# A new order of the first stage's parts on four engines and the DMA queue, and one semaphore per decay buffer

## What is computed

```
h = layernorm(x) * (1 + ca) + sa;  x = x + ga * attention0(h)   # 16 query heads in 4 groups, width 16,
h = layernorm(x) * (1 + cb) + sb;  x = x + gb * (h @ w.T + bias) #   RMS norm and rotation of q and k, causal softmax
h = layernorm(x) * (1 + ca) + sa;  x = x + ga * attention1(h)   # 16 heads of 128, exponential decay by distance
h = layernorm(x) * (1 + cb) + sb;  x = x + gb * (experts(h) + shared(h))   # the best 2 of 8 experts
```

## Time and profile before

| | us |
|---|---|
| median of 3 runs | 1146.86 |
| lowest, highest | 1146.69, 1147.84 |
| the profiled execution, its own time | 1147.24 |
| its span, first to last instruction | 1145.5 |
| first stage, last work ends (B low of batch 2) | 239.05 |
| shift writes end, groups 0, 1, 2, 3 | 41.77, 54.94, 66.25, 81.01 |
| groups 4, 8, 12, 15 | 91.03, 140.55, 190.90, 225.43 |
| granted clock of TensorE, mean (1 is full speed) | 0.968 |

### The profile page before, as it was taken

One profiled execution on the slowest core, in us unless ns is written; L12 is line 12 of the kernel. 1 busy time (PEld: TensorE's weight loads), 2 busy tenths in 40 slices (PEclk: granted clock), 3 DMA queues, 4 the chain that ended last, 5 costly groups with the idle time before them and its releaser, 6 DMA issues. The chain is left out here.

```text
span 1145.5 us, 22304 instructions
## 1 busy us (share of the span) xinstructions
PE 1055.6 (92%) x7524; PEld 919.3 (80%) x7524; DVE 896.3 (78%) x1816; ACT 734.0 (64%) x1398; POOL 334.2 (29%) x335
## 2 busy tenths in 40 slices
PE   5988888869999999999999999999999997979994
PEld 4756666658899899899899898898898986769992
DVE  5798988856788788788788788788788787857765
ACT  4679797766766666666666666666666763615650
POOL 3353544442311201211211111111111244753440
PEclk9799999989999999999999999999999998989997
DMA  7210001010401311321311311221221292834426
GB/s 255 94 52 16 15 6 56 2 50 23 135 20 52 112 46 47 106 46 51 101 50 52 98 53 53 97 54 53 86 65 54 91 37 100 329 99 120 124 89 225
DMA packets 70264, 92.13 MB, mean 80 GB/s; under 512 B 22609, under 2 KB 50385, under 8 KB 69170
## 3 DMA queue, kind: packets, MB, share of 16 engines
q1 hardware_dynamic: 66786, 81.83, 25.7%
q0 software_dynamic: 3408, 9.39, 2.2%
HBM read 46.35 MB, written 42.75 MB: 78 GB/s over the span
## 5 line engine op out<-in xcount | busy, mean ns | idle before, releaser
L1551 PE MATMUL all_psum<-all_h_parts,attn_wp 128*128 128x512 f32 x1140 | 296.2, 395 | 0.0
L1551 PEld LDWEIGHTS all_psum<-all_h_parts,attn_wp 128*128 128x128 f32 x1140 | 209.1, 188 | 39.5
L1723 ACT CAST attn_pp<-attn_p 128x512 fp32r<-128x512 f32 (+3 forms) x256 | 117.4, 459 | 188.4 <-DVE attn_p L1831 186.2
L1812 DVE TENSOR_TENSOR attn_pp<-attn_p,attn_pp 128x512 fp32r<-128x512 f32 (+3 forms) x256 | 198.0, 773 | 6.5 <-ACT attn_pp L1723 6.5
L1970 POOL TENSOR_TENSOR all_gate<-all_gate,attn_sq 128x512 f32<-128x512 f32 x64 | 84.7, 1324 | 368.6 <-ACT attn_sq L1734 368.5
L1630 PE MATMUL all_psum<-attn_qkp 128*128 128x512 f32 (+3 forms) x768 | 164.6, 323 | 3.7 <-DVE attn_qkp L1812 3.7
L1577 PE MATMUL all_psum<-attn_pp,attn_vp 128*128 128x512 f32 (+3 forms) x768 | 163.3, 321 | 1.1 <-DVE attn_pp L1812 0.5
L1577 PEld LDWEIGHTS all_psum<-attn_pp,attn_vp 128*128 128x128 f32 x768 | 128.9, 189 | 21.6 <-issue 1.5
L1630 PEld LDWEIGHTS all_psum<-attn_qkp 128*128 128x128 f32 x768 | 124.1, 189 | 12.4 <-issue 4.3
L1831 DVE TENSOR_TENSOR attn_p<-all_psum,attn_mask 128x512 f32<-128x512 f32 (+3 forms) x256 | 123.4, 482 | 3.6 <-PE all_psum L1630 2.5
L1054 DVE TENSOR_REDUCE front_top<-all_psum 128x2 f32<-128x256 f32 (+3 forms) x128 | 99.3, 814 | 16.4 <-PE all_psum L695 15.1
(11 more groups left out here) (375 smaller groups left out, 1892.9 us busy)
## 6 DMA issues: line engine op xcount, KB each, us to landing
...
```

The costliest lines, as they stand in the source:

```text
L1551: last = nc.tensor.matmul(out, wp[:, a, k, col:col + P], hh[:, c, k, b * S:(b + 1) * S], start=(m == 0), stop=(m == 5))
L1723: nc.scalar.copy(pp[:, u % 2, 0, cols], p[:, cols]).then_inc(p_hi, 1)
L1812: nc.vector.tensor_tensor(out, whole, high.bitcast(F32), ALU.subtract).then_inc(ready, 1)
```

## The change

The tables and the two strings get other values. The parts and their instructions are the same ones. The semaphore `stored` becomes ten, one for each decay buffer; a wait for all stores becomes ten waits, and the wait before a buffer is written again is for that buffer's own store. The diff (the hunks that follow the tables are whole):

```diff
-PROLOGUE_AT = {"L stats": (0, 0), "L rstd": (0, 0), "L norm": (0, 10), "xt": (0, 13), "pj0": (0, 17), "pj1": (0, 17),
-               "sq": (1, 1), "ss": (1, 9), "std": (1, 12), "krot": (1, 13), "rms": (1, 14), "qn": (1, 18),
-               "rot": (2, 0), "va": (2, 8), "rope": (2, 11), "kt": (2, 12), "qt0": (2, 17)}
-POST_AT = {"A add": (0, 0), "at": (0, 7), "A rstd": (0, 11), "out": (0, 12), "A stats": (0, 18), "A norm": (1, 8),
-           "ta": (1, 14), "A low": (1, 16), "bias": (1, 17), "B add": (2, 4), "ff": (2, 11), "B stats": (2, 14),
-           "B rstd": (2, 16), "B low": (3, 3), "B norm": (3, 7), "tb": (3, 14)}
-FIRST_AT = {"dec12": (0, 0), "diag0": (0, 0), "dec10": (0, 4), "dec11": (0, 6), "dec13": (1, 8), "dec14": (1, 19),
-            "diag1": (2, 0), "diag2": (2, 4), "gb0": (2, 8), "gb1": (2, 16), "w ffn": (3, 1), "diag3": (3, 2),
-            "gb2": (3, 5), "dec15": (3, 9), "gb3": (3, 20)}
-OPENING = ("L_stats.0 dec.0 mod.0 L_rstd.0 cast dec.1 L_norm.0 dec.2 dec.3 xt.0 dec.4 pj.0.0 "
-           "mod_copy.0 pj.0.1 mod.1 std.0 kt.0 dec.5 sq.0 rms.0 va.0 dec.6 mod.2 krot.0 rp.0 qt.0.0 "
-           "dec.7 rp.1 s mod_copy.1 mod_copy.2 rp.2 dec.8 s s s dec.9 s s s s s mod.3 mod_copy.3")
+PROLOGUE_AT = {"L stats": (0, 0), "L rstd": (0, 0), "L norm": (0, 10), "sq": (0, 12), "xt": (0, 13), "pj0": (0, 16),
+               "pj1": (1, 0), "krot": (1, 3), "ss": (1, 9), "std": (1, 9), "rms": (1, 13), "qn": (1, 14),
+               "rot": (1, 15), "kt": (2, 9), "rope": (2, 12), "qt0": (2, 15), "va": (3, 16)}
+POST_AT = {"A add": (0, 4), "at": (0, 6), "A rstd": (0, 9), "out": (0, 10), "A stats": (1, 1), "A norm": (1, 8),
+           "A low": (1, 11), "ta": (2, 1), "bias": (2, 6), "ff": (2, 12), "B add": (2, 14), "B stats": (2, 17),
+           "B norm": (3, 13), "tb": (3, 16), "B rstd": (3, 18), "B low": (3, 19)}
+FIRST_AT = {"dec10": (0, 2), "dec11": (0, 6), "dec12": (0, 7), "diag0": (0, 13), "dec13": (0, 14), "dec14": (1, 4),
+            "gb0": (2, 0), "gb1": (2, 11), "diag1": (2, 11), "w ffn": (2, 19), "diag2": (3, 0), "gb2": (3, 1),
+            "diag3": (3, 3), "dec15": (3, 11), "gb3": (3, 20)}
+OPENING = ("mod.0 cast L_stats.0 L_rstd.0 dec.0 L_norm.0 xt.0 mod_copy.0 dec.1 pj.0.0 pj.0.1 std.0 "
+           "mod.1 sq.0 dec.2 kt.0 dec.3 dec.4 mod.2 dec.5 va.0 rms.0 krot.0 rp.0 qt.0.0 rp.1 rp.2 s "
+           "dec.6 dec.7 mod_copy.1 mod_copy.2 s s dec.8 s s s s s s mod.3 mod_copy.3 dec.9")
 LATE_AT = 1
-INTERLEAVE = "ONNNOONONNNOOONNNOOO"
+INTERLEAVE = "ONNOONNNONNOONONNOOO"
...
@@ -506,7 +506,7 @@
         cond_loaded, slope_loaded, x_loaded = n.sem("cond_loaded"), n.sem("slope_loaded"), n.sems("x_loaded", B)
         wmod_loaded, wqkv_loaded, wo_loaded = n.sems("wmod_loaded", 4), n.sem("wqkv_loaded"), n.sem("wo_loaded")
         bias_loaded, tables_loaded, ffn_loaded = n.sem("bias_loaded"), n.sem("tables_loaded"), n.sem("ffn_loaded")
-        next_loaded, kt_loaded, stored = n.sem("next_loaded"), n.sems("kt_loaded", G0), n.sem("stored")
+        next_loaded, kt_loaded, stored = n.sem("next_loaded"), n.sems("kt_loaded", G0), n.sems("stored", len(decays))
         cond_exp, cond_step, scond_ready = n.sem("cond_exp"), n.sem("cond_step"), n.sem("scond_ready")
         zeroed, ident_set, const_ready, half_set = n.sem("zeroed"), n.sem("ident_set"), n.sem("const_ready"), n.sem("half_set")
         eps_set, kt_zeroed = n.sem("eps_set"), n.sem("kt_zeroed")
@@ -593,7 +593,8 @@
                 for ev in order:
                     if ev[0] == "dec":
                         sp.wait_ge(decay_masked, ev[1] + 1)
-                        sp.dma_start(t["decay_dram"][ev[1]], decays[ev[1] % len(decays)]).then_inc(stored, 16)
+                        sp.dma_start(t["decay_dram"][ev[1]], decays[ev[1] % len(decays)]).then_inc(
+                            stored[ev[1] % len(decays)], 16)
                     elif ev[0] == "kt":
                         b = ev[1]
                         if b == 1:
@@ -608,7 +609,8 @@
                             for r in range(R0):
                                 sp.dma_start(kt[r * SLOT:(r + 1) * SLOT, g, r, :], kall[g * SLOT:(g + 1) * SLOT, b % 2, :]
                                              ).then_inc(kt_loaded[g], 16)
-                sp.wait_ge(stored, 16 * H1)
+                for i in range(len(decays)):
+                    sp.wait_ge(stored[i], 16 * len(range(i, H1, len(decays))))
                 sp.dma_start(t["wraw"][:, :].rearrange("p (k n) -> p k n", k=KT), d["w1p"][0]).then_inc(next_loaded, 16)
                 sp.wait_ge(next_loaded, 16)
                 for b in range(B):
@@ -769,7 +771,7 @@
                     if kind == "dec":
                         h = ev[1]
                         if h >= len(decays):
-                            act.wait_ge(stored, 16 * (h - len(decays) + 1))
+                            act.wait_ge(stored[h % len(decays)], h // len(decays) * 16)
                         nc.scalar.activation(decays[h % len(decays)], dist[:, :], ACT.Exp, scale=nslope[:, h:h + 1]
                                              ).then_inc(decay_made, 1)
                     elif kind == "cast":
@@ -805,7 +807,8 @@
                         norm_l.scalar_norm(nc, act, ev[1])
                     elif kind == "A norm":
                         if ev[1] == 0:
-                            act.wait_ge(stored, 16 * H1)
+                            for i in range(len(decays)):
+                                act.wait_ge(stored[i], 16 * len(range(i, H1, len(decays))))
                         norm_a.scalar_norm(nc, act, ev[1])
                     elif kind == "B norm":
                         norm_b.scalar_norm(nc, act, ev[1])
@@ -1071,7 +1074,8 @@
                         if b == 2:
                             dve.wait_ge(aot_done, b - 1)
                         if b == B - 1:
-                            dve.wait_ge(stored, 16 * H1)
+                            for i in range(len(decays)):
+                                dve.wait_ge(stored[i], 16 * len(range(i, H1, len(decays))))
                         nc.vector.tensor_tensor((ao[:, b % 2] if b < B - 1 else left.ao)[:, :, h:h + R0, :], o[:, :, :, 0:D0],
                                                 rden[:, :, :].unsqueeze(3).to_broadcast([P, TB, R0, D0]),
                                                 ALU.mult).then_inc(ao_done, 1)
```

## The result

The change makes the kernel slower: 1152.14 us median (20 runs, 1147.08 to 1154.47) against 1147.8 of the kernel before beside it (20 runs), a ratio of 1.0035 with a 95% interval of 1.0026 to 1.0045, or +4.0 us. The forecast was 1142.9, the range 1138.0 to 1148.5. Timed again it gave 1.0029 (run 12). The profiled execution took 1151.35 us, its span is 1149.6.

What follows compares the result with a forecast made beforehand. The prediction saw the first stage bound by waits moving among PE, DVE and ACT, nearly level and none at its limit. Its terms summed to -3.95 us from 1147.24, giving 1142.9 us on the median's footing, range 1138.0 to 1148.5.

Steps and rivals of the forecast that it cites:

- opening and group 1: First stage's start: score reductions 0.7 us earlier, one score tile in DVE's 3.27 us hole; -1.9 us together.
- weights' cast, groups 2 to 4: Group 3 to 4: DVE's 1.64 us wait for the feed forward weights' cast shrinks by 1.0, half kept; -0.5 us.
- group 5: Batch 1: out.0 and s.5.3.0 ahead of xt.2, pj.2.1 behind q2.5; the shift comes 0.7 earlier, -0.65 us.
- groups 8 and 9: First of two batches where a tile moves ahead of tb and B norm and tb come later; net -0.4 us.
- groups 10 and 11: ta moves from group 10 to 11, qn from 11 to 10; DVE is solid with the same work, 0.
- groups 12 and 13: Second of two batches where a tile moves ahead of tb and B norm and tb come later; net -0.4 us.
- last batch: Groups 14 and 15: a 0.89 us wait goes, but ta.2 puts ff.2 0.5 us later; -0.4 us.
- semaphores: One wait becomes ten on ACT, SP and DVE's last-batch pv; waits already met, 1.4 us at most, +0.3 taken.
- tail: Stage's end: B norm 2 moves behind one more exponential, kq's banks are free 0.9 us sooner, tb.2 waits for both; 0.
- rival (b): Gains at one group's shifts are lost in the next wait for pv; -2.0 us left, 1144.9; chance 0.14.
- rival (c): TensorE's clock falls to half at std in three batches; up to 4.8 us lost, 1147.7; chance 0.06.
- Rival (a): In 15 groups DVE's second score tile, behind pv and an st tile, is late; +3.5, about 1150.4; chance 0.13.

Runs made afterwards that it cites:

- run 6: The changed kernel with only std set back to its earlier place behind the exponentials; ratio 1.0039 to the kernel before.
- run 4: The changed kernel with B norm and tb set back to their places of before; ratio 1.0015 to the kernel before.
- Run 10: The kernel before with the new opening, first batch's parts and ten semaphores, plus seven PSUM banks passed over to restore batches 1 to 3's banks; ratio 1.0008.
- run 17: The changed kernel with the second score tile of seven groups ahead of pv again and 21 tiles in other banks; ratio 1.0025 to the kernel before.

## Why the prediction was wrong

By its own steps, with the measured terms from the two profiled executions:

| term | forecast | measured |
|---|---|---|
| opening and group 1 | -1.9 | -0.8 |
| weights' cast, groups 2 to 4 | -0.5 | +0.7 |
| group 5 | -0.65 | -0.5 |
| groups 6 and 7 | 0 | +0.9 |
| groups 8 and 9 | -0.4 | +1.9 |
| groups 10 and 11 | 0 | +1.55 |
| groups 12 and 13 | -0.4 | +2.1 |
| last batch | -0.4 | -0.55 |
| semaphores | +0.3 | inside the others |
| tail | 0 | 0 |

**Groups 8, 9, 12 and 13.** The step that failed is the walk "shift 12 0.8 earlier, end of pv.11 0.2 later, and then 0.5 won until shift 13". Counted from shift 11, the first clause was right and more (1.0). The end of pv.11 came 0.75 later (13.48 us for 12.73). From there to shift 13, 0.3 was won at full clock (8.3 us in run 6 for 8.7), but the changed kernel took 10.0. So the term that was mis-sized first is the end of pv: ACT's last exponential of group 11 ended 12.75 us after shift 11 for 12.01, and 0.5 of that is its longer standing for PE's tiles (1.66 for 1.14), for which the prediction has no term. It is not B norm and tb as such: run 4 has them back and ends pv.11 at 13.53. The prediction had written "pv.11 needs the last of these", and PE did wait 1.92 us and DVE 2.66, since shift 12 came sooner and the exponentials later. At full clock the two pairs of groups would have come out at +0.1 and +0.4, for -0.4 each: 1.3 us of error. That is rival (b), won and given back, and it alone would not have left the range.

**The clock** is the greatest single error: 3.4 us in these groups. The forecast had it at nothing. It stood as rival (c) with a chance of 0.06 and at one place, std. TensorE does stand there, 2.42 us, and the clock is at half behind it in groups 6 and 10; but it is at half also behind the waits for pv.7 and pv.11. What was held against the rival, that the clock stayed at 1.00 in groups 9 and 10 of the kernel before, was weak evidence: PE's waits there were 0.37 and 1.90, not 1.92 and 2.42, and group 13 shows that one and the same wait can be followed by either clock. The price taken, 1.6 us for a stretch that DVE does not cover, was right.

**Groups 10 and 11 at 0** failed on "what it has to do is the same". DVE's work was the same, but its waits grew by 1.1 us, and a write that takes 0.7 to 0.8 us when it is alone took 2.31 for 1.93 beside POOL, whose chain begins with the part that was moved later, "the right way by the busy times".

**The opening**: DVE's reductions did start at 34.98, as forecast, for 35.58, but waited 0.21 and 0.16 for PE afterwards; shift 0 came at 41.82, for 41.77, and the whole -0.8 is group 1's. DVE's hole of the earlier trace rows had been closed, and opened again at the tiles. PE, at half clock as before, began its score tiles at 34.28 for 33.84, behind ACT's copy. Run 10 says the same: nothing won.

**What was right**: one tile ahead of the hole in group 1, the wait for the weights at 0.69, group 5, groups 8 and 12, group 14 (8.7 for 10.2), the semaphores' small price, the tail. The wait for the weights did shrink as forecast, but groups 2 to 4 grew all the same. Rival (a), the second tile behind pv, is not the cause as far as run 17 shows: with the tile set back in seven groups the ratio is 1.0025.

**What stays open**: what it costs that ta was moved; how much the stretches in groups 6 and 10 cost; what brings the clock down in one profile and not in another; and why groups 2 and 3 take 1.0 longer (DVE waits 1.99 and 0.56 for 1.50 and 0.45 in group 2, which is 0.6 of it).
